# Four steps of a decoder layer moved to GpSimd, three orders for each engine, and the loads reordered

## What is computed

```python
def _apply_kernel(x, orf):                       # random features of q and k
    proj = einsum('bhld,md->bhlm', x, orf) / d_k ** 0.25
    norm = sum(x * x, axis=-1, keepdims=True) / (2.0 * sqrt(d_k))
    return (exp(proj - norm) + 1e-6) / sqrt(m)
# linear attention: 16 heads of 16, m = 64 features
q_phi, k_phi = _apply_kernel(q, orf), _apply_kernel(k, orf)
out = (q_phi @ (k_phi.T @ v)) / (q_phi @ sum(k_phi))        # then @ Wo.T + bo
x = _layernorm(x + out)
x = _layernorm(x + softmax((x Wq)(ctx Wk).T / 4) (ctx Wv))  # per head
def _act_quant(x):
    scale = 127.0 / clip(max(abs(x), axis=-1, keepdims=True), 1e-05)
    return clip(round(x * scale), -128.0, 127.0) / scale
gate, up = silu(aq(x) @ wq(w_gate).T), aq(x) @ wq(w_up).T   # 256 -> 1024
x = _layernorm(x + aq(gate * up) @ wq(w_down).T)            # 1024 -> 256
```

## Time and profile before

| | |
|---|---|
| median of 3 runs | 504.59 us (503.21 to 504.9) |
| the profiled execution | 507.6 us, of it the span of the program 505.9 us |
| busy: PE / DVE / ACT / POOL | 437.2 / 450.7 / 429.1 / 365.0 us |
| the same as a share of the span | 86% / 89% / 85% / 72% |
| TensorE clock granted, mean | 0.972 of full |
| read from and written to HBM | 17.31 MB and 4.19 MB |

### The profile page before, as it was taken

One profiled execution on the slowest core, in us unless ns is written; L12 is line 12 of the kernel. 1 busy time (PEld: TensorE's weight loads), 2 busy tenths in 40 slices (PEclk: granted clock), 3 DMA queues, 4 the chain that ended last, 5 costly groups with the idle time before them and its releaser, 6 DMA issues.

```text
span 505.9 us, 18665 instructions
## 1 busy us (share of the span) xinstructions
PE 437.2 (86%) x6566; PEld 304.7 (60%) x6566; DVE 450.7 (89%) x1355; ACT 429.1 (85%) x908; POOL 365.0 (72%) x789
## 2 busy tenths in 40 slices
PE   4568888889899999999999999999999988866541
PEld 2235666666677667677767776777777766543220
DVE  4667786889999999999999999999999998999771
ACT  2247788979999999999999999999999998866632
POOL 1447766768888888888888888888888876754332
PEclk9979899999999999999999999999999999999975
DMA  7666556776666666666666666666666777532212
GB/s 180 235 127 110 121 125 116 110 136 94 137 136 140 137 142 138 139 140 145 145 145 145 145 135 141 136 138 143 137 140 130 136 137 138 76 74 53 54 42 62
DMA packets 192644, 64.07 MB, mean 127 GB/s; under 512 B 172384, under 2 KB 192352, under 8 KB 192608
## 3 DMA queue, kind: packets, MB, share of 16 engines
q1 hardware_dynamic: 190080, 60.46, 58.2%
q10 hardware_dynamic: 2528, 3.15, 1.7%
HBM read 17.31 MB, written 4.19 MB: 43 GB/s over the span
## 4 chain that ended last, share of the span: by engine, by line
PE 56%; ACT 15%; DMA 11%; DVE 7%; issue 5%; POOL 3%; SPq 1%; ACTq 0%; POOLq 0%; DVEq 0%
PE bank L1129 11%; PE bank L1333 8%; PE bank L1360 4%; PE bank L1304 3%; PE bank L1181 3%; PE bank L1223 3%; DMA tT<-pkT 3%; DMA ffn_ld<-in_L_ffn_w_down_dram 3%; ACT pT L629 3%; PE bank L1143 3%; ACT pT L628 2%; DMA tT<-nmT 2%; PE bank L1238 2%; PE bank L1320 2%; ACT x L556 2%
## 5 line engine op out<-in xcount | busy, mean ns | idle before, releaser
L1129 PE MATMUL bank<-wq_hi,xT 128*128 128x512 f16 (+1 forms) x256 | 72.1, 337 | 4.0 <-DVE vv L814 2.6
L432 POOL TENSOR_TENSOR ve<-mv,lneps 128x1 f32<-128x1 f32 x96 | 19.2, 200 | 67.8 <-DVE mv L864 52.7
L436 POOL TENSOR_TENSOR rs<-ve,mhalf 128x1 f32<-128x1 f32 x96 | 54.7, 569 | 0.0
L628 ACT ACTIVATE pT<-bank 128x512 f32<-128x512 f32 x64 | 37.9, 592 | 12.6 <-PE bank L1294 10.6
L944 DVE SCALAR_TENSOR_TENSOR g<-th,bank 128x512 f32<-128x512 f32 x64 | 42.9, 671 | 3.9 <-ACT th L651 3.7
L556 ACT ACTIVATE x<-y,nmr,rs 128x256 f32<-128x256 f32 x64 | 39.8, 621 | 7.4 <-DVE y L1005 3.8
L895 DVE TENSOR_REDUCE negm<-bank 128x4 f16<-128x512 f32 x64 | 43.5, 679 | 2.8 <-PE bank L1258 2.7
L896 DVE TENSOR_REDUCE negm<-bank 128x4 f16<-128x512 f32 x64 | 43.6, 681 | 0.0
L1360 PE MATMUL bank<-downT,hqT 128*128 128x256 bf16 x256 | 34.3, 279 | 10.3 <-DMA hqT<-hq 10.3
L575 ACT ACTIVATE phk<-bank 128x512 f32<-128x512 f32 x64 | 39.3, 616 | 4.6 <-PE bank L1148 4.6
L1129 PE MATMUL bank<-wq_lo,xT 128*128 128x256 f16 (+1 forms) x128 | 43.0, 336 | 0.0
(11 more groups left out here) (184 smaller groups left out, 1574.7 us busy)
## 6 DMA issues: line engine op xcount, KB each, us to landing
xs<-in_x_dram SPq DMA_DIRECT2D x32, 128.0 KB, 2.2
cs<-in_ctx_dram SPq DMA_DIRECT2D x32, 128.0 KB, 2.2
xr<-in_x_dram SPq DMA_DIRECT2D x32, 128.0 KB, 2.2
out_dram<-ot SPq DMA_DIRECT2D x32, 128.0 KB, 1.8
ffn_ld<-in_L_ffn_w_gate_dram ACTq DMA_DIRECT2D x1, 1024.0 KB, 8.7
ffn_ld<-in_L_ffn_w_up_dram ACTq DMA_DIRECT2D x1, 1024.0 KB, 11.5
ffn_ld<-in_L_ffn_w_down_dram ACTq DMA_DIRECT2D x1, 1024.0 KB, 13.7
pkAT<-pkA SPq DMA_TRANSPOSE x64, 3.2
```

What stands on the lines that cost most here:

```text
L436: g.tensor_tensor(rs[n - 1][:, :], ve[n - 1][:, :], mhalf[:, :], ALU.pow).then_inc(done[f"pw{n}"], 1)
L628: sc.activation(pT[:, grp, 0, :, :], even.rearrange("p (c t) -> p c t", c=4), ACT.Exp, scale=0.25)
L1129: last = T.matmul(o, xT[:, 2 * part + c, :], w[:, c, cols], start=(n == 0), stop=(n == 5))
```

## The change

Five things change, and nothing in what is computed.

1. `nhi`, `nlo` and `qnt` go from VectorE to GpSimd, and `ot_` goes from ScalarE to GpSimd. `ot_` now subtracts the mean and multiplies by rs in one step, so `rs3` no longer makes nm and nmr.
2. Each engine has three orders: `ramp`, `iteration` and `drain`. In the ramp and the drain each step has an offset of its own (`lead`, `trail`). The loop of the chip runs over fewer tiles.
3. The order within the loop, the lags and the PSUM banks are other numbers. On TensorE the waits that free a bank stand for each of the first and last tiles by name (`only_at`), and in the loop as `wait_looped`.
4. SP loads x of tile 0 first, then Wq, Wk, Wv, x of tile 1, the biases, w_down; w_gate and w_up come later, behind two more loads of x. ScalarE's queue no longer loads them.
5. The small constants and the clearing of buffers on VectorE all come ahead of the weights' preparation.

```diff
+        def lead(step, i, lag, until):
+            t = i - lag
+            if 0 <= t < until:
+                step(t, t % 2)
+        def trail(step, i, lag, since):
+            t = i - lag
+            if since <= t < TILES:
+                step(t, t % 2)
-        def run(eng, iteration, lags, first):
+        def run(eng, ramp, iteration, drain, ramps, first, last, drains):
+            for i in range(*ramps):
+                ramp(i)
+            iteration(first - 2, 0)
+            iteration(first - 1, 1)
+            with eng.Fori(first, last - 1, 2) as i:
                 iteration(i, 0)
                 iteration(i + 1, 1)
-            for i in range(TILES, TILES + lags):
-                iteration(i, i % 2)
+            for i in range(*drains):
+                drain(i)
@@ sync
+            load_first(0)
             for n, w in enumerate((Wq, Wk, Wv)):
                 sp.dma_start(wld[:, n, :, :], w.rearrange("(o p) i -> p o i", p=P)).then_inc(w_in[n], 16)
+            load_first(1)
+            load_gate = partial(load_matrix, 0, w_gate, 8)
+            load_up = partial(load_matrix, 1, w_up, 8)
+            load_down = partial(load_matrix, 2, w_down, 2)
             def kT(t, par):
-                wait_ahead(sp, t, par, ("lo", 0), ("nlo", 0), ("phk0", -1))
+                wait_ahead(sp, t, par, ("lo", 0), ("phk1", -1))
@@ gpsimd
+            def nhi(t, par):
+                wait_ahead(pool, t, par, ("nr", 0), landings=(("kT", -1), ("qT", -1),))
+                g.tensor_scalar(norm_hi, nrm[:, :, :], 1.0, 0.0, ALU.mult, ALU.add).then_inc(done["nhi"], 1)
+            def nlo(t, par):
+                wait(pool, "nhi", t)
+                g.tensor_tensor(norm_lo, nrm[:, :, :], norm_hi, ALU.subtract)
             def rs3(t, par):
-                rstd(3, t, par)
+                g.tensor_tensor(ve[2][:, :], mv[2][:, par, 1:2], lneps[:, :], ALU.add).then_inc(done["ve3"], 1)
+                wait(pool, "ve3", t)
+                g.tensor_tensor(rs[2][:, :], ve[2][:, :], mhalf[:, :], ALU.pow).then_inc(done["rs3"], 1)
+            def ot_(t, par):
+                wait_ahead(pool, t, par, ("rs3", 0), landings=(("out", -2),))
+                g.tensor_scalar(ot[:, par, :], y[2][:, par, :], mv[2][:, par, 0:1], rs[2][:, :], ALU.subtract,
+                                ALU.mult).then_inc(done["ot"], 1)
+            def qnt(t, par):
+                wait_ahead(pool, t, par, ("ar", 0))
+                g.tensor_scalar(xm[:, par, :], x2[:, par, :], arec[:, :], MAGIC, ALU.mult, ALU.add).then_inc(
+                    done["qnt"], 1)
@@ vector, loop
             def iteration(i, par):
+                go(bs3, i, par, 9)
+                go(m0, i, par, 5)
+                go(y3, i, par, 9)
+                go(at, i, par, 3)
+                go(qk_, i, par, 0)
...
-            run(dve, iteration, 9, 12)
+            run(dve, ramp, iteration, drain, (-14, -1), 14, 30, (11, 22))
@@ tensor, one step as an example
             def dn(t, par):
                 first_time(pe, t, 0, ffn_out, 6)
+                only_at(pe, t, 0, "kvm", 6)
...
+                wait_looped(pe, "kvm", t, 6)
                 wait_moved(pe, "hqT", t, par)
-            run(pe, iteration, 9, 10)
+            run(pe, ramp, iteration, drain, (-65, -9), 14, 30, (-7, 4))
```

## The result

The changed kernel takes **511.95 us** in the median of four runs (510.94 to 512.42) against 504.35 of the kernel before on the same chip (503.21 to 504.9): a ratio of 1.0151, 95% interval 1.0127 to 1.0175. The forecast was 482 us with a range of 473 to 498, so the time lies outside it and on the other side of no change. The profiled execution has a span of 510.1 us, against 505.9 before. The profiled execution of before, at 507.6 us, lay some 3 us above the median of its runs, that of the changed kernel, at 512.19, only 0.2 above; so the two profiles show 4.2 us of the 7.6 us between the medians.

The account below looks back on a forecast made before the run. VectorE was taken to set the loop's 13.06 us a tile, with ScalarE just behind. From the 505.9 us span, loop 9.5, head 4, ramp 4 and drain 5 left 483.4, a 485.1 us run, forecast 482 us; range 473 to 498.

Parts of the forecast that it names:

- GpSimd's price for ot: Third layer norm's last step on GpSimd: 0.37 us like the one-tensor step xhi, upper end 0.69 us.
- GpSimd's sum: GpSimd's work per tile in the loop: 11.16 us busy before, 12.0 after, likely 12.3 with sequencing, just under 12.57.
- VectorE being full, a tile can fall to 12.57: Loop: 0.49 us a tile leaves VectorE, so 13.06 falls to 12.57 us; 9.5 us counted over 20 periods.
- at nothing: TensorE in the loop: same work, other banks and order, costed at no time; three more waits would eat the gain.
- Head: Start of the run: x loaded first brings the first qk near 12 us, the second near 22; gain 4 us.
- Ramp and drain: Tiles before and after the loop: own orders remove waiting, 4 us (0 to 9) in the ramp, 5 (0 to 10) in the drain.
- the third rival: Loop gains as said, but ramp and drain are latencies no order shortens: 491.5 us, chance 0.2 (488 to 495).
- From the profiled run to the median: End of the sum: the median of runs lies 3.0 us below the profiled run, so 485.1 becomes 482 us.
- The rule on the shared port: Ramp and loop: certain VectorE steps and GpSimd steps block each other whole through a shared port pair; no size given.
- The first (GpSimd becomes the bound): Loop: GpSimd sets 12.9 to 13.1 us a tile if the moved steps cost their upper ends; 495 us, chance 0.14.
- The second: Loop: GpSimd waits as well as works, 1.6 us a tile of waits, period 13.9; 511 us, chance 0.08.
- What would show it: Signs in the new profile, among them period 12.5 to 12.7 us; wrong if GpSimd's qnt or ot is over 0.6 us.

Follow-up runs that it names:

- e2: The changed kernel with ot still on GpSimd but written as y times rs plus nmr, nm and nmr made as before the change: 503.26 us.
- h1: The kernel before with VectorE's work cut: the two maxima of the hidden layer look at half of their columns: 501.62 us.
- h3: The kernel before with VectorE's hidden-layer maxima and ScalarE's hidden-layer scalings both cut to half of their columns: 494.31 us.
- m2: The changed kernel with ot as y times rs plus 0, mean left out, and work cut on TensorE, VectorE, ScalarE and GpSimd: 494.17 us.
- k1: The kernel before with x of tile 0 loaded ahead of the projection weights, x of tile 1 behind them, GpSimd's bo wait at first use: 504.93 us.
- k2: The kernel before with nhi and nlo moved to GpSimd behind lo, and ot moved there as multiply and add ahead of hq0: 521.06 us.
- f1: The kernel before with only nhi, nlo and qnt moved from VectorE to GpSimd, ahead of xqf and lo: 541.52 us.
- e1: The changed kernel with ot alone back on ScalarE, behind thi and ahead of p0, nm and nmr back on GpSimd: 672.18 us.

## Why the prediction was wrong, step by step

- **GpSimd's price for ot: the step that made it slower.** It was taken as a one-tensor step like xhi, 0.37 us, with 0.69 as the upper end. It measured 1.20. My bounds looked at the elements, the number of tensors and the scalars; what decides is the pair of operations. "The per-partition scalars are the open point" was the wrong one of two open points: they cost 0.07 us each. The trace of before held a warning at most in that no row of it had this pair. The rest of GpSimd's sum was sound: with the four prices as measured, 12.3 becomes 13.3 us, and the period was 13.42. This term is worth 8.7 us of the time: 6.8 of the loop's 18.3 us miss (tile 8 to tile 31 is 311.9 us in the changed kernel, 305.1 in e2), most of the rest in the drain, 102.4 us against 101.0 in e2.
- **"VectorE being full, a tile can fall to 12.57": the step that cost most.** Most of the remaining 18.3 - 6.8 = 11.5 us of the loop's miss. Two things were wrong in it. VectorE was full, but so were ScalarE and TensorE, as the earlier trace rows said (99% each); h1 shows that 0.5 us off VectorE gives 0.12. I relieved ScalarE too, by the same change, and then didn't ask for TensorE: it was costed "at nothing" though its 256.76 us busy are 12.9 us a tile, above the 12.57 that I forecast. (Busy is no exact measure of its work: in h3, with the same matmuls, it is 12.67 us a tile. That is still above 12.57.) h3 shows where the order of before stops with both engines relieved, at 12.72. And in the new order the loop ends at 12.91 with a cheap ot, by waits that no single engine's work explains (m2: 12.78 with all four cut). In e2 the period's gain of 0.07 us is worth 1.6 us over these 23 tiles where 9.5 were forecast, which makes 7.9 of the 11.5 us.
- **The joints between the three orders: a term that the sum didn't have.** The other 3.6 us are the net of what lies outside the steady part, above all where the ramp's order passes into the loop's and the loop's into the drain's. In e2 the qk steps of tiles 15 and 16 start 14.2 and 14.3 us behind the one ahead of them, those of tiles 30 and 31 13.7 and 14.3, where the kernel before has 12.9 to 13.2. No run looked into what holds them there.
- **Head: right at both marks, and for a reason only half right.** First qk 12.66 (12 forecast), second 22.88 (22). The reason given, that x comes early, isn't enough: with it alone the first qk starts at 18.16 (k1). The order of VectorE's ramp was needed.
- **Ramp and drain: 9 us forecast, next to nothing found.** By tile 8 head and ramp have gained 5.1 us, of which the second qk already had 2.6; by tile 17 it is 3.3. VectorE is idle 26.1 us from 20 to 140 us (40 - 27.62 + 80 - 66.26), where under 19 was to be seen, and before it was 22.8; it has less work there, and waits as much. The drain gained nothing: 102.4 us from the last qk on, 101.9 before, in part at a lower TensorE clock (0.91 granted from 440 to 480 us, 1.00 before). Both terms were sums of idle time of one engine, of which I took a share with no row that showed the share could go. In the last 100 us both kernels have the same long waits, for the transposed hq (7.4 us at the longest in both) and for the last down projection (6.2 in both), a chain of one tile that neither order shortened; the third rival said this.
- **From the profiled run to the median: 3 us.** The sum took 3.0 us off because the profiled run of before lay that much above its median. The changed kernel's lay 0.2 above, so this step is the rest of the 30 us between 482 and 511.95.
- **The rule on the shared port.** In the ramp of the changed kernel xlo takes 1160 ns in the mean (4 of them) against 0.68 in the loop, and nhi 583 against 0.34, so GpSimd's steps are stretched there again, as nf's was in the earlier trace rows. The rows tell beside what: in the kernel before, nf at 26.91 us takes 0.72 us while VectorE's reduction over 2048 elements runs from 26.41 to 28.69, and nf at 43.77 takes 1.57 while a tensor_scalar step on 2048 elements runs from 43.01 to 44.78. In the loop nothing is stretched. The Trainium skill's rule ("SBUF — State Buffer", section Who interferes with whom) agrees with where this is seen; no run here took it apart.
- **The rivals.** The first (GpSimd becomes the bound) is what happened, and its size was still wrong: it had the period at 12.9 to 13.1 by upper ends of 0.69, and 495 us. The second gave 511 us, near the measured time, but by waits of 1.6 us a tile that the changed kernel doesn't have; its mechanism is k2's. The right number there was chance. That the kernel gets slower had 0.08 of the chances; with GpSimd's slack at 0.3 us of 12.57 by my own sum, and one unseen operation in it, it should have had several times that.
- **What would show it.** "It would be wrong if GpSimd's row of qnt or ot is over 0.6 us" was the sign to look for, and ot's row gives it at once.

The range was too narrow because the unknown price was bounded by rows of other operations as if these were its ends, and because no rival put together what came together: a dear step, neighbours as full as VectorE, and a ramp and drain that give nothing.

## What to carry to other kernels

In a loop where three engines are 99% busy, taking work off one is worth only the distance to the next: before costing a move, set every engine's busy time per tile beside the forecast period, and doubt a forecast that lies below the largest. A step that an engine's trace doesn't show has no upper end in other steps' rows; on GpSimd the pair of operations alone changed a step of 256 elements from 0.55 to 1.22 us, and writing the same formula as multiply and add gave 8.7 us back. Idle time of an engine is room only if the wait behind it goes: put work into a list ahead of the step that others wait for and it costs nearly its full length (f1: +1.4 us in the ring, +1.2 us a tile). The queue that issues the transfers is such a list too: when a step moves, look at what its store holds up (e1).

## What the runs showed of the hardware that was not expected

- GpSimd, two operations of one tensor with scalars, 128 x 256 fp32: multiply-add 0.40 us with constants (there written as bf16), 0.48 with one per-partition scalar, 0.55 with two; subtract-multiply 1.07 with constants and 1.22 with two. Add-multiply over 1024 elements: 1.05 us.
- Taking 0.4 to 0.5 us a tile off each of two engines gave 0.12 and 0.03 us alone and 0.33 together, at a full granted TensorE clock in all of them.
- A step of 0.6 us at another place of ScalarE's list made the store behind it late, and that held up SyncE's next transfers: 7 us a tile (e1: period 20.48 us against 13.42, at a granted TensorE clock of 0.82 from 140 to 400 us).
